# Expert and shared convolutions from f16 halves in place of f32, and a new order of GpSimd's queue

## What is computed

```python
def _L0_conv_ref(x, ...):                       # mixture of experts
    rw, topk_i = ...                            # router on mean and std of x: 2 of 8 experts per image
    shared = silu(group_norm(conv1x1(x, shared_w, groups=8)))
    fused = conv3x3(x, fused_w, groups=8)       # 8 groups of 16 channels in, 128 out each
    eo = take_along_axis(fused, topk_i)         # expert e is the output of input group e
    en = group_norm(eo) * gam + bet
    return shared + (silu(en) * rw).sum(axis=1)

def _L1_conv_ref(x, ...):                       # window attention, 8 heads, windows of 8 x 8
    q, k, v = windows(qkv_w @ x + qkv_b)
    attn = softmax(q @ k.T / 4 + bias)
    out = attn @ v + depthwise_conv7x7(v)
    return proj_w @ out + proj_b

x = x + _L0_conv_ref(_gn(x), ...)
x = x + _L1_conv_ref(_gn(x), ...)
```

## Time and profile before

| | |
|---|---|
| Time, 3 runs | 764.18, 764.08, 758.54 us; median 764.08 |
| Profiled execution | 761.66 us, of which the span from first to last instruction is 759.7 us |
| Busy: TensorE, VectorE, ScalarE, GpSimd | 645.3, 565.1, 453.1, 188.5 us |
| Mean granted TensorE clock | 0.963 of full |
| HBM traffic | 147 GB/s over the span |

### The profile page before, as it was taken

One profiled execution on the slowest core, in us unless ns is written; L12 is line 12 of the kernel. 1 busy time (PEld: TensorE's weight loads), 2 busy tenths in 40 slices (PEclk: granted clock), 3 DMA queues, 4 the chain that ended last, 5 costly groups with the idle time before them and its releaser, 6 DMA issues.

```text
span 759.7 us, 18623 instructions
## 1 busy us (share of the span) xinstructions
PE 645.3 (85%) x6926; PEld 388.0 (51%) x6926; DVE 565.1 (74%) x1124; ACT 453.1 (60%) x758; POOL 188.5 (25%) x295
## 2 busy tenths in 40 slices
PE   5426759899989899999999899999999898889892
PEld 3412324655556464656555565646566566444430
DVE  3842656888888888988888888889888977332692
ACT  1123555768676776867686767768676852355451
POOL 4042133140404223131404042231312101000182
PEclk9997868999999999999999999999999999999997
DMA  8433183555646574746556464747452242465194
GB/s 329 180 132 98 59 223 108 174 158 153 184 129 200 145 206 147 213 128 200 160 151 189 128 199 144 215 138 210 134 168 86 82 147 72 139 222 181 20 257 167
DMA packets 53871, 121.13 MB, mean 159 GB/s; under 512 B 10131, under 2 KB 26646, under 8 KB 53782
## 3 DMA queue, kind: packets, MB, share of 16 engines
q1 hardware_dynamic: 41814, 78.87, 32.9%
q0 software_dynamic: 8800, 28.45, 15.3%
q10 hardware_dynamic: 3168, 12.62, 4.3%
HBM read 70.58 MB, written 40.93 MB: 147 GB/s over the span
## 4 chain that ended last, share of the span: by engine, by line
PE 47%; ACT 25%; issue 12%; DVE 6%; DMA 5%; POOL 1%; ACTq 1%; POOLq 1%; SPq 0%; DVEq 0%
PE g L1067 10%; PE g L1085 7%; ACT y L518 6%; PE t L1135 4%; PE g L1095 4%; PE g L1263 4%; ACT vp L563 4%; PE pv L1150 4%; PE s L1124 3%; PE s L1254 3%; DMA vt<-x 3%; ACT y L514 3%; ACT pt L584 3%; PE t L1254 3%; ACT L518 2%
## 5 line engine op out<-in xcount | busy, mean ns | idle before, releaser
L1067 PE MATMUL g<-xsh,wsel 96*128 96x512 f32 x256 | 132.6, 647 | 23.8 <-ACT y L514 13.1
L514 ACT ACTIVATE y<-g 128x512 f32<-128x512 f32 x96 | 55.6, 596 | 92.0 <-PE g L1067 75.6
L875 DVE TENSOR_REDUCE mx<-s 128x8 f32<-128x512 f32 x128 | 87.0, 679 | 26.8 <-PE s L1124 26.8
L811 DVE BATCH_NORM_STATS2 st<-y 128x6 f32<-128x512 f32 x96 | 64.6, 686 | 51.7 <-ACT y L514 51.6
L1135 PE MATMUL t<-ident,less 128*128 128x128 f32 x512 | 79.3, 278 | 15.7 <-ACT pt L584 15.0
L879 DVE TENSOR_TENSOR less<-s,mx 128x512 f32<-128x512 f32 x128 | 88.5, 691 | 4.4
L1067 PEld LDWEIGHTS g<-xsh,wsel 96*128 96x128 f32 x256 | 46.7, 200 | 76.3 <-issue 63.8
L1135 PEld LDWEIGHTS t<-ident,less 128*128 128x128 f32 x512 | 62.5, 145 | 44.7 <-DVE less L879 21.7
L584 ACT ACTIVATE pt<-t 128x512 f32<-128x512 f32 x128 | 74.6, 595 | 14.2 <-PE t L1135 13.7
L1150 PE MATMUL pv<-vp,pt 128*64 128x34 f32 x2048 | 79.2, 222 | 3.0 <-DVE ot L893 2.8
L1150 PEld LDWEIGHTS pv<-vp,pt 128*64 128x64 f32 x2048 | 71.4, 140 | 4.0 <-ACT pt L584 2.9
(11 more groups left out here) (155 smaller groups left out, 1119.7 us busy)
## 6 DMA issues: line engine op xcount, KB each, us to landing
xsh<-xs POOLq DMA_DIRECT2D x64, 210.0 KB, 3.7
xs<-xn ACTq DMA_DIRECT2D x16, 578.0 KB, 2.9
vt<-x SPq DMA_DIRECT2D x4, 2048.0 KB, 17.6
xin<-x POOLq DMA_DIRECT2D x16, 512.0 KB, 4.7
sq_d<-qhl SPq DMA_DIRECT2D x32, 256.0 KB, 2.4
sk_d<-khl SPq DMA_DIRECT2D x32, 256.0 KB, 2.2
...
```

Of the source, the lines that this page charges most:

```text
L514: act.activation(y[:, k, h * HALF:(h + 1) * HALF], g[at][:, :], ACT.Identity).then_inc(g_free[at], 1)
L811: last = v.bn_stats(st[:, 2 * k + h, :], y[:, k, h * HALF:(h + 1) * HALF])
L875: v.tensor_reduce(mx[:, p % 2, :], scored, AX.X, ALU.max).then_inc(sem["s_max"], 1)
L1067: last = mm(g[at][:, :], wsel[:, k - 1, C * dy:C * dy + C], xsh[:, k - 1, dy + 16 * h:dy + 16 * h + 16, 0:W], start=(dy == 0), stop=(dy == 1))
```

## The change

The convolutions of the first block take f16 operands. The normalised image, times 16, is split into a high and a low f16 half (`xhl`), the expert weights, times 64, into halves as well; the products high-high, low-high and high-low are summed in PSUM, and the copy out of PSUM divides by 1024. The low-low product is left out.

- **An expert's half image** is four f16 matmuls of 512 columns: three (one for each row shift) on 128 partitions, in which 16 channels x 3 column shifts stand for high x high, 48 for low image x high weights and 32 for high x low weights of two columns, and a fourth on 48 partitions (`xb`, `wsb`) for the third column of high x low. The shared one is three f16 matmuls.
- **ScalarE** normalises image b + 3 into `vn` (f32) and casts that into the high half, both behind the copy and the q and k passes of part 0. **GpSimd** subtracts to get the low half and issues the save of `xs`, now 16 bits wide and with two copies in turn.
- **GpSimd's list in step b** becomes: low half and save of b + 3; split of v of b (it was that of b + 1 at the end); weights of b + 3, two DMAs for each expert; inverse roots of b + 2; rows of b + 3, four DMAs for each expert; gammas and betas; load of x; second inverse root.
- **At the start**, SP loads all expert weights behind x, ScalarE scales and casts them, GpSimd makes the low halves, and SP writes them to DRAM in the layout of the matmuls, 32 DMAs. The loads of the first two images by GpSimd stand ahead of that. ScalarE's first normalising pass stands between the router's square root and exponentials.

```diff
+PADDED = (H + 2) * WPAD
+RUN = PADDED - 2
+RUN2 = (H - 1) * WPAD + W
+XSCALE = 16.0
+WSCALE = 64.0
+EXW = 9 * C
...
-        xsh = sb("xsh", [SH, TOP, H + 1, WPAD])
+        xa = sb("xa", [C, TOP, H + 2, WPAD], F16)
+        xb = sb("xb", [SHR, TOP, H, WPAD], F16)
...
-        xn = sb("xn", [C, H + 2, WPAD])
+        xhl = sb("xhl", [C, 2, H + 2, WPAD], F16)
...
-        wsel = sb("wsel", [SH, TOP, 2 * C])
+        wsa = sb("wsa", [C, TOP, 3 * C], F16)
+        wsb = sb("wsb", [SHR, TOP, C], F16)
+        wsh = sb("wsh", [C, 2, C], F16)
...
+            sp.dma_start(wx32, wx).then_inc(sem["wx_loaded"], 16)
+
+            def save_experts():
+
+                sp.wait_ge(sem["wx_hi"], 2)
+                for copy in range(2):
+                    for e in range(E):
+                        dst = wa_d[e, SHR * copy:SHR * copy + SHR].rearrange("(c d) n -> c (d n)", d=3)
+                        sp.dma_start(dst, wxh[GC * e:GC * e + GC, :]).then_inc(sem["wx_saved"], 16)
+                sp.wait_ge(sem["wx_low"], 2)
+                for e in range(E):
+                    dst = wa_d[e, 2 * SHR:C].rearrange("(c d) n -> c (d n)", d=2)
+                    sp.dma_start(dst, wxl[GC * e:GC * e + GC, 0:6 * C]).then_inc(sem["wx_saved"], 16)
+                    dst = wb_d[e].rearrange("(c d) n -> c (d n)", d=3)
+                    sp.dma_start(dst, wxl[GC * e:GC * e + GC, 6 * C:EXW]).then_inc(sem["wx_saved"], 16)
...
+            pool.wait_ge(x_loaded[3], 16)
+            for j in range(2):
+                pool.dma_start(xin[:, j, :], x[j].rearrange("c h w -> c (h w)")).then_inc(xin_loaded[j], 16)
+            pool.wait_ge(sem["wx_hi"], 2)
+            nc.gpsimd.tensor_tensor(wxl, wx32[:, 0:EXW], wxh, ALU.subtract).then_inc(sem["wx_low"], 1)
+            nc.gpsimd.tensor_tensor(wsh[:, 1, :], wx32[:, EXW:], wsh[:, 0, :], ALU.subtract).then_inc(sem["wx_low"], 1)
...
+            def save_xn(j):
+
+                pool.wait_ge(sem["xn_done"], 2 * j + 2)
+                nc.gpsimd.tensor_tensor(xhl[:, 1, 1:H + 1, 1:W + 1], vn[:, :].rearrange("p (y x) -> p y x", x=W),
+                                        xhl[:, 0, 1:H + 1, 1:W + 1], ALU.subtract).then_inc(sem["xn_low"], 1)
+                pool.wait_ge(sem["xn_low"], j + 1)
                 if j > 1:
-                    pool.wait_ge(sem["sum_shared"], j - 1)
-                pool.dma_start(xin[:, j % 2, :], x[j].rearrange("c h w -> c (h w)")).then_inc(xin_loaded[j % 2], 16)
-
-            def load_rows(j):
+                    for k in range(TOP):
+                        pool.wait_ge(rows_loaded[k], ROW_DMAS * (j - 1))
+                pool.dma_start(xs[j % 2], xhl[:, :, :, :].rearrange("p t h w -> p (t h w)")).then_inc(sem["xn_saved"], 16)
+
+            def load_weights(j, k):
+
+                if j:
+                    for h in range(2):
+                        wait_ready(pool, f"y{k + 1}", j - 1, h)
+                else:
+                    pool.wait_ge(sem["wx_saved"], 16 * 4 * E)
+                    pool.wait_ge(sem["setup_dve"], 31)
+                e = pool.value_load(rnum[0:1, 4 * j + 2 + k:4 * j + 3 + k], min_val=0, max_val=E - 1)
+                pool.dma_start(wsa[:, k, :], wa_d[bass.ds(e, 1)].rearrange("e p n -> p (e n)")).then_inc(rows_loaded[k], 16)
+                pool.dma_start(wsb[:, k, :], wb_d[bass.ds(e, 1)].rearrange("e p n -> p (e n)")).then_inc(rows_loaded[k], 16)
+
+            def load_rows(j, k):
 
                 pool.wait_ge(sem["xn_saved"], 16 * j + 16)
...
+                e = pool.value_load(rnum[0:1, 4 * j + 2 + k:4 * j + 3 + k], min_val=0, max_val=E - 1)
+                mine = e * (GC * 2 * PADDED) + j % 2 * (C * 2 * PADDED)
+
+                def rows(offset, step, count, run):
+                    return bass.AP(xs.tensor, mine + offset, [[2 * PADDED, GC], [step, count], [1, run]])
+
+                wide = xa[:, k, :, :].rearrange("p h w -> p (h w)")[:, 0:RUN]
+                pool.dma_start(wide[0:SHR], rows(0, 1, 3, RUN)).then_inc(rows_loaded[k], 16)
+                pool.dma_start(wide[SHR:2 * SHR], rows(PADDED, 1, 3, RUN)).then_inc(rows_loaded[k], 16)
+                pool.dma_start(wide[2 * SHR:C], rows(0, 1, 2, RUN)).then_inc(rows_loaded[k], 16)
+                pool.dma_start(xb[:, k, :, :].rearrange("p h w -> p (h w)")[:, 0:RUN2], rows(2, WPAD, 3, RUN2)
+                               ).then_inc(rows_loaded[k], 16)
...
 
                 if has3:
-                    load_rows(b + 3)
+                    save_xn(b + 3)
+                split_v(b)
+                if has3:
+                    load_weights(b + 3, 0)
+                    load_weights(b + 3, 1)
                 if has2:
                     rsqrt(b + 2, 0, 3)
                 if has3:
+                    load_rows(b + 3, 0)
+                    load_rows(b + 3, 1)
                     choose_affine(b + 3)
                 if b + 4 < B:
                     load_x(b + 4)
                 if has2:
                     rsqrt(b + 2, 1, 1)
-                if has1:
-                    split_v(b + 1)
-
-            load_x(0)
-            load_x(1)
+
+            save_xn(0)
+            for k in range(TOP):
+                load_weights(0, k)
+            for k in range(TOP):
+                load_rows(0, k)
             choose_affine(0)
-            load_rows(0)
-            load_rows(1)
+            save_xn(1)
             rsqrt(0, 0, 3)
+            for k in range(TOP):
+                load_weights(1, k)
+                load_rows(1, k)
             choose_affine(1)
             load_x(2)
             rsqrt(0, 1, 1)
+            save_xn(2)
             rsqrt(1, 0, 3)
+            for k in range(TOP):
+                load_weights(2, k)
+                load_rows(2, k)
             choose_affine(2)
-            load_rows(2)
             load_x(3)
             rsqrt(1, 1, 1)
-            split_v(0)
...
+            act.wait_ge(sem["wx_loaded"], 16)
+            act.activation(wx32, wx32, ACT.Identity, scale=WSCALE).then_inc(sem["wx_scaled"], 1)
+            act.wait_ge(sem["wx_scaled"], 1)
+            act.activation(wxh, wx32[:, 0:EXW], ACT.Identity).then_inc(sem["wx_hi"], 1)
+            act.activation(wsh[:, 0, :], wx32[:, EXW:], ACT.Identity).then_inc(sem["wx_hi"], 1)
...
+                elif j < 3:
+                    act.wait_ge(sem["xn_low"], j)
+                else:
+                    act.wait_ge(sem["v_turned"], j - 2)
+                act.activation(vn[:, :], xin[:, j % 2, :], ACT.Identity, bias=gnx[:, 1, j:j + 1],
+                               scale=gnx[:, 0, j:j + 1]).then_inc(sem["xn_done"], 1)
+
+            def high_xn(j):
+
+                act.wait_ge(sem["xn_done"], 2 * j + 1)
+                if j == 0:
                     act.wait_ge(sem["setup_pool"], 1)
-                    sc, sh = gn0[:, 0, 0:1], gn0[:, 1, 0:1]
                 else:
                     act.wait_ge(sem["xn_saved"], 16 * j)
                     for h in range(2):
                         wait_ready(act, "y0", j - 1, h)
-                    sc, sh = gn0[:, 0, j:j + 1], gn0[:, 1, j:j + 1]
-                act.activation(xn[:, 1:H + 1, 1:W + 1], xin[:, j % 2, :].rearrange("p (y x) -> p y x", x=W), ACT.Identity, bias=sh, scale=sc).then_inc(sem["xn_done"], 1)
-
-                act.wait_ge(sem["xn_done"], j + 1)
-                if j:
-                    act.wait_ge(sem["rows_loaded"], 32 * TOP * j)
-                act.dma_start(xs, xn[:, :, :].rearrange("p h w -> p (h w)")).then_inc(sem["xn_saved"], 16)
+                act.activation(xhl[:, 0, 1:H + 1, 1:W + 1], vn[:, :].rearrange("p (y x) -> p y x", x=W),
+                               ACT.Identity).then_inc(sem["xn_done"], 1)
...
                     if p != 5 or not has1:
                         exponential(b, p)
-                    if has3 and p == 0:
-                        normalise(b + 3)
                     if p < 2:
                         if has2:
                             copy_y(b + 2, 2, (p,))
                         if has1:
                             high_qk(b + 1, 0, p)
                             high_qk(b + 1, 1, p)
+                    if has3 and p == 0:
+                        normalise(b + 3)
+                        high_xn(b + 3)
...
                 if k == 0:
-                    pe.wait_ge(sem["xn_done"], j + 1)
+                    pe.wait_ge(sem["xn_done"], 2 * j + 2)
+                    pe.wait_ge(sem["xn_low"], j + 1)
                 else:
-                    pe.wait_ge(sem["rows_loaded"], 32 * TOP * (j + 1))
-                    pe.wait_ge(sem["chosen_w"], 16 * TOP * (j + 1))
+                    pe.wait_ge(rows_loaded[k - 1], ROW_DMAS * (j + 1))
                 for h in halves:
                     at, n = BANK_USE[f"y{k}", j, h]
                     pe.wait_ge(g_free[at], n)
                     if k == 0:
-                        last = mm(g[at][:, :], w[:, WSH:WSH + C], xn[:, 1 + 16 * h:17 + 16 * h, 1:W + 1], start=True,
```

(12 more changed lines are left out.)

70 lines of the change are left out of this document (37 added, 33 removed).

## The result

| | before | changed |
|---|---|---|
| median of 4 runs | 764.1 us (758.5 to 767.0) | 787.2 us (780.5 to 788.6) |
| profiled execution, its span | 761.7, 759.7 us | 787.1, 785.0 us |
| mean granted clock of that span | 0.963 | 0.944 |
| a middle step | 34.8 us, every one | 35.6 to 39.7, mean 37.1 us |

The account below looks back on a forecast made before the run. With TensorE relieved, a loop through GpSimd's queue was taken to bound the steps: 761.7 + 14 for thirteen steps + 0 for the start - 1 for the last gives 774.7, said as 775 us; range 756 to 789.

Parts of the forecast that it names:

- The loop through GpSimd: Middle steps: ScalarE, GpSimd and VectorE legs in series take 35.85 us against 34.8, 1.1 us longer a step; chance 0.52.
- the first rival: Middle steps: GpSimd is in time, VectorE sets the pace at 32.7 us a step, 734 us; chance below 757 us 0.14.
- the clock: Rival: TensorE idles in the new wait and falls to half clock, up to 1 us a step, 788 us; shared chance 0.12.
- The +14: Thirteen middle steps: the longer loop adds 14 us in all, within +3 to +31 us.
- a longer leg: Middle steps: GpSimd's leg exceeds its forecast, time above 783 us; chance 0.12 together with clock spells.
- the first leg of the loop: Pair 0, ScalarE and TensorE: from the copy's end through convolution, q and k to the image's cast, 6.25 us.
- the new wait: Middle steps: VectorE waits 3.2 us for GpSimd's inverse roots, in place of old waits of 2.1 us.
- the forecast's own range of 768 to 783: Whole kernel: the time in us if GpSimd's loop behaves as forecast; chance 0.52.
- The start: Before the steps: later expert weights and half-price convolution taken to cancel, 0 us, within -2 to +5.
- the lower of the two prices: Start: SP's 32 small DMAs at 0.42 us each, landed near 50 us, against 0.63 each, near 56.
- Half a convolution: TensorE: four f16 matmuls for half an expert's convolution take 1.0 us, within 0.9 to 1.24, in place of 1.79.
- VectorE's floor: Middle steps: VectorE's work in order plus its remaining wait for ScalarE's copy allows no less than 32.6 to 32.8 us.

Follow-up runs that it names:

- Runs 1 and 2: Changed kernel with, in each GpSimd step, the weight loads behind the inverse roots (749.1 us), or the split of v ahead of the subtract (751.1 us).
- run 3: Changed kernel with both GpSimd edits: split of v ahead of the subtract, and weight loads behind the inverse roots; 736.4 us.
- run 6: Changed kernel with ten unread f16 matmuls on TensorE, only in the gap ahead of the values of pair 4; 785.5 us.
- run 7: Changed kernel with five unread f16 matmuls on TensorE, only ahead of the second expert's convolution in pair 0; 772.2 us.
- run 10: The kernel of run 7 with GpSimd's cast of v made twice in place of once, ahead of the inverse roots; 789.3 us.
- All eleven variants: The eleven follow-up kernels, each measured against the kernel before; medians from 729.7 to 789.3 us.
- runs 3 and 7 to 11: run 3, run 7, run 10; run 3 with cast of v thrice, 752.3 us; that with VectorE's squares reading PSUM, 739.0; run 3 with copy before window pass, 729.7.

## Why the prediction was wrong

From the profiles, the spans differ by 785.0 - 759.7 = 25.3 us:

| part | forecast | measured |
|---|---|---|
| up to the end of the last copy before the steps (119.93, now 113.39) | 0 | -6.5 |
| thirteen steps | +14 | +29.4 |
| last step (32.6, now 31.7) | -1 | -0.9 |
| from the last window pass to the end (156.9, now 160.2) | 0 | +3.3 |

- **The loop through GpSimd was right**, term by term (35.91 against 35.85), and so was its cause. Runs 1 and 2 take one part each out of it and get steps of 34.1 and 33.5 us; run 3 takes both and gets the first rival's kernel, 736 us for 734. Steps at a granted clock of 1.00, 35.6 to 35.9 us, are within 0.3 of the forecast.
- **The step that failed is the clock, which the sum put at nothing.** The +14 has no term for it. As a rival it was said to cost "up to 1 us" a step, since waits for ScalarE in pair 6 swallow most of a spell, and it shared a chance of 0.12 with a longer leg. Eight of the thirteen steps have a spell in pair 0, and take between 37.2 and 38.1 us; summed, they stand 12.9 us above 35.9 each, 1.6 us a step. Most of that falls in pair 0, not in pair 6: the spell begins with the second expert's convolution and the q and k projections, which are the first leg of the loop, where nothing swallows it (7.85 against 6.20). This gap, 1.3 us of waiting for ScalarE's copy, was not in the forecast. The one that was, made by the new wait, stands ahead of the values of pair 4 (the forecast had it one pair later, ahead of the projection of turned v). In the change it brings a second spell in two of the eight steps and the only one in two others, and filling it does nothing for the time (run 6); filling the other gives 772 us (run 7), inside the forecast's own range of 768 to 783. But it is not a harmless gap: in run 10 it brings the spells. The rival's sum, 788, was right within 1 us, partly by chance, since the start came 6.5 us early and one step of 39.7 us was not in it.
- **What stays open of the clock** is why one such gap is followed by a fall and the next is not. At pair 0 the same 1.30 us with TensorE busy 2.11 of the 4 us around it has both outcomes in the change (444 and 255.62 us); at pair 4 gaps of 2.5 us do and do not bring one. Run 7 shows that the spells in pair 0 need the gap ahead of it, not what else they need. The counts of steps are from one profiled execution of each kernel.
- By the Trainium skill (TensorE: Matmul & The Clock Gate, "HAM oscillation") idle time that comes back in every pass of a loop throttles the array in every pass. The page's case is a wait for a DMA each time, longer than the two gaps here. The trace agrees in that spells come back, at 0.57, in eight of thirteen steps; it does not agree in the "every": three further steps have the same 1.3 us at pair 0 and no spell behind it.
- **One step of 39.7 us** stands in the sum as well, 3.8 above the loop. There GpSimd issues the first load of weights 2.2 us late behind its split (no gap in the step shown above), TensorE then waits 3.85 us at pair 4 and is busy 1.12 of the 4 us from 350, and a spell follows. All eleven variants have a gap of 1.9 to 3.7 us ahead of that load in this one step, between 326 and 353 us, and the kernel before has none. Its cause was not found, and no run was made for it.
- **The start** was wrong in sign. It was taken that GpSimd's queue is the chain there, 3 to 6 us late. The 32 small DMAs took 0.42 to 0.48 us each on SP, the lower of the two prices, and were issued by 48.9; the loads of weights at 53.49 waited only for the router's numbers. The last convolution before the steps began at 107.77 without waiting for rows, where it had waited 5.08 us.
- **The end.** 156.9 and 160.2 us lie both within 155.0 to 161.9, which runs 3 and 7 to 11 show for the same code. The 3.3 us are not shown to be the change's.
- **Smaller terms.** Half a convolution was put at 1.0 us and measures 1.05 to 1.07; the cast at 1.25 and takes 1.06; the rest of GpSimd's queue is within 0.3 together. TensorE was put near 80% of a step and is busy 30.9 of 35.9 us, 86%. VectorE's floor was put at 32.6 to 32.8 us and is 32.9 in run 3. The new wait was put at 3.2 us and is 1.7, for the held sum of L885. None of these bears on the result.
